# The least norm of queries and keys: a maximum on VectorE, or a relu and a biased logarithm on ScalarE

## What is computed

```python
def l2norm(t):
    return t / jnp.clip(jnp.linalg.norm(t, axis=-1, keepdims=True), 1e-12)

def _layer(x, wqkv, qs, ksc, wo, lg, lb, w1, b1, w2, b2):
    q, k, v = jnp.split(shift_token(x) @ wqkv, 3, axis=-1)   # 8 heads of 64
    q = l2norm(q) * qs
    k = l2norm(k) * ksc
    q, k = rotary_xpos(q, k)
    o = local_attention(q, k, v)          # windows of 64, each sees itself and the one before
    x = x + o @ wo
    h = layer_norm(shift_token(x)) * lg + lb
    a, g = jnp.split(h @ w1 + b1, 2, axis=-1)
    return x + (a * gelu(g)) @ w2 + b2
```

## Time and profile before

| | |
|---|---|
| median of three runs | 1183.93 us (1179.61 to 1187.25) |
| the profiled execution: time, span of its instructions | 1180.76 us, 1179.0 us |
| TensorE, matmuls | 996.0 us busy (84% of the span) |
| VectorE | 827.2 us (70%) |
| ScalarE | 717.2 us (61%) |
| GpSimd | 390.5 us (33%) |
| mean granted clock of TensorE | 0.93 |

### The profile page before, as it was taken

One profiled execution on the slowest core, in us unless ns is written; L12 is line 12 of the kernel. 1 busy time (PEld: TensorE's weight loads), 2 busy tenths in 40 slices (PEclk: granted clock), 3 DMA queues, 4 the chain that ended last, 5 costly groups with the idle time before them and its releaser, 6 DMA issues.

```text
span 1179.0 us, 22117 instructions
## 1 busy us (share of the span) xinstructions
PE 996.0 (84%) x8272; PEld 595.4 (50%) x8272; DVE 827.2 (70%) x1381; ACT 717.2 (61%) x1500; POOL 390.5 (33%) x251
## 2 busy tenths in 40 slices
PE   5069997248997679999999979898989999999996
PEld 3023324112323466766766656555556666667662
DVE  3078823348863688888988877767777889888861
ACT  3027773106784477777677666656565776777762
POOL 5000005000000755445544434243434455445420
PEclk9589998659999699999999989999999999999998
DMA  2960000680000411011100101000000111011100
GB/s 56 132 122 10 1 1 19 102 106 8 2 1 1 101 27 24 20 24 24 29 20 19 28 8 26 6 19 15 19 15 19 25 24 29 16 24 37 34 10 18
DMA packets 38268, 36.01 MB, mean 31 GB/s; under 512 B 11478, under 2 KB 30224, under 8 KB 38160
## 3 DMA queue, kind: packets, MB, share of 16 engines
q1 hardware_dynamic: 34708, 31.46, 14.2%
q10 hardware_dynamic: 3456, 3.15, 1.2%
HBM read 15.41 MB, written 4.21 MB: 17 GB/s over the span
## 4 chain that ended last, share of the span: by engine, by line
PE 46%; DVE 13%; issue 4%; ACT 3%; POOL 2%; DVEq 0%; POOLq 0%
PE psum L1162 7%; PE psum L1134 5%; PE psum L1094 5%; PE psum L1073 4%; PE psum L1037 4%; PE psum L1170 4%; PE psum L1047 3%; PE psum L1083 3%; PE psum L1039 3%; PE psum L1038 3%; DVE f_NM L1424 3%; DVE f_A L1392 2%; DVE f_BS L1396 2%; DVE f_SS L1403 2%; DVE f_PT L1416 2%
## 5 line engine op out<-in xcount | busy, mean ns | idle before, releaser
L966 POOL TENSOR_TENSOR f_A<-f_A,f_BS 128x1024 f32<-128x1024 f32 x64 | 150.9, 2357 | 229.4 <-DVE f_BS L1396 229.3
L500 DVE TENSOR_REDUCE a_M<-psum 128x1 f32<-128x512 f32 x256 | 159.8, 683 | 60.1 <-PE psum L430 59.8
L430 PE MATMUL psum<-a_KS,a_QS 128*128 128x512 bf16 x256 | 102.6, 409 | 76.4 <-DMA a_KS<-minus_ones 72.6
L971 POOL TENSOR_TENSOR f_A<-f_A,f_RN 128x1024 f32<-128x1024 f32 x64 | 121.8, 1903 | 107.9 <-ACT f_RN L1282 107.2
L547 ACT ACTIVATE a_PT<-psum 128x1024 f32<-128x1024 f32 x128 | 126.4, 1018 | 50.9 <-PE psum L452 50.7
L1271 ACT ACTIVATE f_PW<-psum,f_NM 128x128 f32<-128x128 f32 x512 | 138.5, 381 | 14.5 <-DVE f_NM L1424 11.6
L1392 DVE TENSOR_TENSOR f_A<-psum,cos 128x512 f32<-128x512 f32 x128 | 87.7, 685 | 48.1 <-ACT f_SQ L1237 47.5
L1424 DVE TENSOR_REDUCE f_NM<-psum 128x4 f32<-128x512 f32 x128 | 81.9, 679 | 54.7 <-PE psum L1073 54.7
L1094 PE MATMUL psum<-f_VS,f_PT 128*64 128x65 f32 x1024 | 82.1, 229 | 38.6 <-DVE f_PT L1416 17.4
L1237 ACT ACTIVATE f_SQ<-psum 128x512 f32<-128x512 f32 x128 | 75.3, 607 | 61.4 <-PE psum L1039 57.1
L1094 PEld LDWEIGHTS psum<-f_VS,f_PT 128*64 128x64 f32 x1024 | 68.6, 140 | 71.6 <-issue 43.0
(11 more groups left out here) (173 smaller groups left out, 1971.8 us busy)
## 6 DMA issues: line engine op xcount, KB each, us to landing
f_VS<-f_V SPq DMA_DIRECT2D x112, 130.0 KB, 2.3
parts<-a_PRT ACTq DMA_DIRECT2D x24, 128.0 KB, 2.4
a_QS<-parts SPq DMA_DIRECT2D x8, 256.0 KB
a_KS<-parts SPq DMA_DIRECT2D x8, 256.0 KB
a_QS<-parts SPq DMA_DIRECT2D x4, 384.0 KB
a_KS<-parts SPq DMA_DIRECT2D x4, 384.0 KB
raw<-L_ffn_wqkv_dram SPq DMA_DIRECT2D x2, 768.0 KB, 6.5
a_XT<-L_attn_a_x_dram SPq DMA_DIRECT2D x4, 256.0 KB, 4.1
```

Source lines behind the costliest of these rows:

```text
L430: nc.tensor.matmul(psum[:, take("tile", 8 * unit + k), :], QS[:, n, h + k // 4, P * qt:P * qt + P], KS[:, n, h + k // 4, :], start=True, s ...
L500: nc.vector.tensor_reduce(M[:, u % 4, k // 4, k % 4:k % 4 + 1], psum[:, bank("tile", i), :], AX_X, ALU.max)\
L966: nc.gpsimd.tensor_tensor(A[:, k % 2, :, :], A[:, k % 2, :, :], BS[:, k % 2, :, :], ALU.add)\
L971: nc.gpsimd.tensor_tensor(x, x, RN[:, k % 2, :, None].to_broadcast([P, 2 * HW, DW]), ALU.mult)\
```

## The change

The stage `norm` on ScalarE computes relu(s - 1e-24) into `LN`, signals `clipped`, and takes the logarithm of that plus 1e-24; the two constants are bias columns in `tiny`. The maximum on VectorE goes, and with it VectorE's wait for its own sum. `norm` now waits for `summed_squares`, which the sum on VectorE signals.

```diff
-        g.tiny = sb("tiny", [P, 2 * HW])
+        g.tiny = sb("tiny", [P, 2])
@@ set-up, GpSimd
-                nc.gpsimd.memset(g.tiny[:, :], 1e-24).then_inc(s("eps"), 1)
-                pool.wait_ge(s("eps"), 2)
+                nc.gpsimd.memset(g.tiny[:, 0:1], 1e-24).then_inc(s("eps"), 1)
+                nc.gpsimd.memset(g.tiny[:, 1:2], -1e-24).then_inc(s("eps"), 1)
+                pool.wait_ge(s("eps"), 3)
@@ stream, ScalarE, stage "norm"
                         k = i
+                        act.wait_ge(s("summed_squares"), k + 1)
+                        nc.scalar.activation(LN[:, k % 2, :], SS[:, k % 2, :], ACT.Relu, bias=g.tiny[:, 1:2])\
+                          .then_inc(s("clipped"), 1)
                         act.wait_ge(s("clipped"), k + 1)
-                        nc.scalar.activation(LN[:, k % 2, :], SS[:, k % 2, :], ACT.Ln).then_inc(s("log"), 1)
+                        nc.scalar.activation(LN[:, k % 2, :], LN[:, k % 2, :], ACT.Ln, bias=g.tiny[:, 0:1])\
+                          .then_inc(s("log"), 1)
                         act.wait_ge(s("log"), k + 1)
@@ stream, VectorE, stage "rope"
                                                 AX_X, ALU.add).then_inc(s("summed_squares"), 1)
-                        dve.wait_ge(s("summed_squares"), k + 1)
-                        nc.vector.tensor_tensor(SS[:, k % 2, :], SS[:, k % 2, :], g.tiny[:, :], ALU.max)\
-                          .then_inc(s("clipped"), 1)
```

## The result

The changed kernel takes 1165.13 us (median of six, 1158.78 to 1167.34) against 1185.74 us (six, 1179.61 to 1188.28) for the kernel before: ratio 0.9835, with 0.9813 to 0.9857 as the 95% interval. That is 20.6 us or 1.65% less. The direction was forecast, and the time lies in the range; the gain of 13.7 us that the sum gave was too small by half of itself.

A forecast was written before the change was run, and what follows sets the result against it. TensorE was taken to bound an ordinary group (41.00 of 42.13 us). Gains of 1.8 + 2.0 + 4.9 + 1.8 = 10.5 us, plus 3.2 us of clock, made 13.7: 1183.93 - 13.7 = 1170.2 us, range 1158 to 1182.

The forecast's parts named there:

- Ordinary second tiles: Second tile of ordinary groups: the copy of probabilities starts 0.16 us sooner, then waits for transposes; 11 x 0.16 = 1.8 us.
- Third tiles: Third tile of ordinary groups: VectorE already idles 2.15 us for the scores, so TensorE's 0.81 us wait stays; no gain.
- Attention b, second tile: Four groups with attention b: the layer norm's product (line 1450) starts sooner, limited by an exponential; 4 x 0.5 = 2.0 us.
- Attention b, last tile: Same four groups: the update of X, queued behind the maximum, starts 1.23 us sooner; 4 x 1.23 = 4.9 us.
- Start: First tile 0.5 us of GpSimd's idling, third tile the full stall of 1.3 us; 1.8 us, plus 1.7 us of clock.
- Clock behind X: Slow matmuls after one 2.39 us wait for X would return to the upper clock level once it shortens; 1.5 us.
- ScalarE's addition at nothing: Relu and bias columns on ScalarE, 0.35 us a tile taken (bounds 0.22 to 0.5), costed at nothing for TensorE.
- The norm moved up: GpSimd's line 971 starts some 0.5 us earlier in ordinary tiles; worth nothing beyond the start.
- The full stall gained everywhere: Rival: the whole stall is gained wherever the waits run through sum and maximum; 25.5 us, 1158.4 us; chance 0.14.
- Nothing gained: Rival: freed time becomes waiting for scores and the longer norm on ScalarE eats the rest; 1180 to 1184 us; chance 0.21.
- Table loads: Rival: relu forces two table loads a tile on ScalarE, about 100 us lost, 1284 us; chance 0.05.
- The wait that moves to another VectorE instruction: Rival: another VectorE instruction with SBUF operands meets the stall, taking back the ordinary part; 1173 to 1180 us; no separate chance.

The follow-up runs named there:

- stall at X: Changed kernel with an unused maximum put back on VectorE in four tiles, ahead of the update of X: 1173.42 us, ratio 0.9934.
- `w1_last` early: Changed kernel with VectorE's last product of the hidden block moved ahead of `soften` and `turn_p_2`: 1157.17 us, ratio 0.9778.
- after again: The changed kernel, unaltered, measured once more in a later series against the kernel before: 1166.71 us, ratio 0.9861.
- no least norm: Changed kernel without relu and bias columns, the logarithm taken of the sum of squares itself: 1163.85 us, ratio 0.9839.
- stall in ordinary tiles: Changed kernel with an unused maximum of two SBUF operands put back on VectorE in 52 of 64 tiles: 1164.22 us, ratio 0.985.
- more relus: Changed kernel with three more relus, without effect on values, in every norm on ScalarE: 1171.01 us, ratio 0.9888.
- maximum and relu: Kernel before, keeping its maximum, with the relu and the biased logarithm added behind it on ScalarE: 1181.06 us, ratio 1.0001.
- immediate: Kernel before with the maximum taken against an immediate number, so one SBUF operand instead of two: 1182.52 us, ratio 0.9991.
- new order: Kernel before, maximum kept, with `w1_last` earlier, attention b's features behind the projection and w1 behind scores and second transposes: 1167.77 us, ratio 0.9847.

## Why the prediction was right, and where its size was off

- **Ordinary second tiles, 1.8 us.** Right. The copy starts when the transposes end (0.16 us of standing), and TensorE waits 0.17 us. The two ordinary stretches gained 1.25 us together, and putting the stall back took 1.5.
- **Third tiles, nothing.** Right: the ordinary stretches moved by less than the second tiles alone were to give, and the stalls put back in second, third and all other ordinary tiles took 1.5 us together.
- **Attention b, second tile, 2.0 us.** Right: the wait for `mid` went from 7.1 to 5.1 us.
- **Attention b, last tile, 4.9 us.** 5.3 measured. Four stalls put back here cost 9.2 us by medians, the clock included.
- **Start, 1.8 us and 1.7 of clock.** 3.5 measured. In the changed kernel the multiplication on the first tile (973) starts 0.14 us behind the addition instead of 0.61, and the window of the third tile has the clock at 1.00, beside 0.72 in the earlier trace rows:

```profile
417.00:423.00 6.00, 6.00 (x75) 4.93 (x71) 5.60 (x11) 4.88 (x12) 4.99 (x4) 1.00 0.06 14
```

  The wait there is 1.74 us, and in two other versions with 1.58 us at this place (the stall at X, and `w1_last` early) the clock did fall behind it, for 1.7 us, while in six others with the same 1.58 us it did not. So that the 1.7 us came back whole was partly luck.
- **Clock behind X, 1.5 us.** This is the step that failed, the one I had called least certain, and it failed in size. I took one fall of the clock behind X to be there and three not, and wrote that the slow stretches behind line 1471 stay. In the kernel before and in the one with the stall at X, the rows show that the two belong together: a long stretch behind 1471 with a short wait for X, or a short one with a long wait and a second fall. With the falls behind `mid` counted in, 15 of the 16 such groups of the four kernels with this stall lose 2.7 to 3.4 us of work, and one 4.4. In the five profiled executions of kernels without the stall in these tiles and in the old order (after, after again, no least norm, stall in ordinary tiles, more relus) the four groups lose 7.8 to 8.7 us; in those four with it (before, maximum and relu, immediate, stall at X) 11.7 to 13.3. The term was worth 3.9 us and not 1.5 in the two executions compared, and 3.0 to 5.5 over all of them.
- **The last tiles.** Forecast nothing, 1.8 us in the pair of profiles. This was the clock in that one execution, 1.7 us of work lost there for 3.7 before: the same stretch was 44.20, 44.20 and 44.14 us in the changed kernel again, without the least norm, and with the stalls in ordinary tiles, as before, and the kernel with the maximum in the new order has the shorter loss too. It doesn't belong to the change. Take it out, and the forecast of 13.7 stands against 15.5 us of the profiles.
- **ScalarE's addition at nothing.** Right; 0.40 us a tile, inside the bounds and 0.05 above the value I took. Another 0.65 us a tile cost some 3 to 4 us, most of it in the attention-b groups and not clear of the spread, while the tight place that I named (line 1271) showed nothing.
- **The maximum in the trace.** I wrote that it always comes some 1.2 us into the addition. It begins about 1.1 us into it (0.99 in the earlier trace rows), since the sum begins before the addition, and 3 of the 64 begin under no GpSimd instruction. The mean that was costed is not touched by this.
- **The norm moved up.** Right in the first, second and fourth tile of an ordinary group: line 973 starts 0.14 to 0.31 us behind the addition, for 0.6 us before. In the third tile it waits 4.3 us for the norm, 0.3 more than before, and TensorE doesn't feel it. In all the wait went from 107.2 to 86.2 us.
- **The rule against the move.** The rule of the Trainium skill (ScalarE: Activation LUTs, section "Rules for kernel authors") speaks of the cost per element, and on that the move does lose: 306 ns for 174. The mean of 1255 ns decided.

The rivals. The full stall gained everywhere: shown false by the stalls in 52 tiles. Nothing gained: false. Table loads: false, the counts are unchanged, as the Trainium skill's table of sets has it (ScalarE: Activation LUTs, section "Table sets"). The wait that moves to another VectorE instruction: true for the casts of `Y` at the start, 3.6 us in all, off the path.

By places and clock the profiles thus account for 17.3 us of the streaming phase. The medians differ by 20.6, and in the second series by 15.6 (1182.3 and 1166.71); the intervals of the two ratios meet between 0.9825 and 0.9857, 17 to 21 us. Much of the spread lies ahead of the change: in the fourteen profiled executions the streaming phase starts between 384.9 and 397.2 us, with the same instructions before it. Whether the remaining 3 us of the first series are more than this spread is open. Open, too, is why the stretch behind 1471 is mostly long before (three of four, and three of four with the immediate) and mostly short after: in the kernel with the stall at X it is mostly short as well, so the stall at X is not its cause. The size goes with the instant of the fall. In the nine executions that have this wait, each of the 15 long stretches has the clock fall 0.7 to 1.5 us before the wait on 1471 ends, and each of the 20 short ones at most 0.6 us before its end or up to 1.4 us behind it; the wait is 3.45 to 3.50 us in all of them. That instant differs between groups and between executions of one kernel, and no run here shows what sets it, so part of the 3.9 us may be the chance of the executions profiled. The shorter wait for `mid`, 18 us ahead, is the other thing that this kernel shares with the changed one; it wasn't tried by itself. And with three more relus, a wait for `mid` of 1.55 us, two of the four were long.

## What to carry to other kernels

A small instruction whose mean is many times its minimum is probably waiting, though no table of waits names it; look at what another engine does in the same microseconds. What its removal is worth has to be read at each place, from the next thing that its consumer would wait for: here 4 of 64 stalls held about half of the gain, and 52 next to nothing. Where TensorE's clock falls behind waits, count the lost work of a whole group and not of one wait, since a stall and a slow stretch hide each other, and expect a second change that removes the neighbouring wait to be worth more together with the first than alone.

## What was not expected of the hardware

- A maximum of 128x16 with an immediate, reading one SBUF operand, stalls under GpSimd's addition exactly as one with two does (1255 ns and 1255 ns in the mean, 174 ns at the least), when it begins under a running GpSimd instruction. The two sums with one SBUF operand that began so did not (1207 and 1208 ns, as the others).
- A larger one shows the same: the `tensor_scalar` of line 1454 (128x512, in place) takes 487 ns in the twelve instances that begin with GpSimd standing, and 897 to 900 ns in the four that begin while it runs.
- The stretches at 1.2 GHz behind one and the same wait of 3.45 us come in two sizes, 1.4 to 1.7 us and 2.7 to 3.0 us of work lost, in executions of one kernel: after and after again had the long one in different groups (the second and the third). The Trainium skill (TensorE: Matmul & The Clock Gate, section "What's actually happening") says of the slow matmuls at the start of a kernel that their number varies from run to run. These two executions show the like in the middle of one.
- The clock also fell behind waits of 1.2 us (`w1_last` early, three of four), of 1.58 us, and of 1.77 to 1.90 us for `mid` (six of twelve in the three kernels that have the maximum with an immediate, with a relu, or in the new order), and stayed up behind others of 1.26 to 1.94 us. The length of the wait alone doesn't tell.
